# A layer of gated experts, attention and gated experts on one core: first rows on two queues, router held in TensorE, results stored in halves

## Time and profile before

| | |
|---|---|
| time, median of 3 runs | 471.35 us (469.79 to 471.42) |
| the profiled execution | 470.26 us, span 468.5 us, granted clock 0.993 |
| PE busy | 443.2 us, 95% of the span |
| PEld busy | 377.1 us, 80% |
| DVE busy | 353.5 us, 75% |
| ACT busy | 265.1 us, 57% |
| POOL busy | 281.6 us, 60% |
| moved by DMA | 53.62 MB, 114 GB/s |

### The profile page before, as it was taken

The page is one execution under the profiler, slowest core; times in us unless marked ns, Lnnn a source line. Parts: engine busy times, 40 slices in busy tenths (PEclk is TensorE's granted clock), DMA queues, the critical chain, the costliest instruction groups (busy, mean ns, idle before and its releaser), DMA issues.

```text
span 468.5 us, 9695 instructions
## 1 busy us (share of the span) xinstructions
PE 443.2 (95%) x2959; PEld 377.1 (80%) x2959; DVE 353.5 (75%) x1112; ACT 265.1 (57%) x596; POOL 281.6 (60%) x290
## 2 busy tenths in 40 slices
PE   7999999999999999999899999998899999999992
PEld 3878878888889888879787788887779888887872
DVE  4899996333688978999899999998899743454553
ACT  5965145555766657667533675654285565565630
POOL 4127556777775067713878850777574767763771
PEclk9999999999999999999999999999899999999998
DMA  7991143355422334311113321221443445553332
GB/s 225 366 341 46 55 127 123 99 174 135 127 84 83 92 95 112 109 44 52 57 53 90 96 70 51 69 80 63 124 129 104 135 148 148 152 160 102 95 102 63
DMA packets 74210, 53.62 MB, mean 114 GB/s; under 512 B 9648, under 2 KB 68784, under 8 KB 74160
## 3 DMA queue, kind: packets, MB, share of 16 engines
q1 hardware_dynamic: 65968, 36.19, 26.1%
q0 software_dynamic: 8192, 16.79, 12.1%
HBM read 26.81 MB, written 26.15 MB: 113 GB/s over the span
## 4 chain that ended last, share of the span: by engine, by line
PE 49%; DVE 22%; POOL 12%; issue 8%; DMA 4%; ACT 3%; SPq 0%; POOLq 0%; DVEq 0%; ACTq 0%
PE pool L899 13%; POOL x_sorted L1150 6%; PE gu L847 6%; PE pool L888 6%; PE gu L849 6%; PE gu L848 6%; POOL yg L1170 4%; PE pool L830 3%; DVE X L1236 2%; DVE hs L1213 2%; DVE hs L1217 2%; DVE stats L1247 2%; PE gu L806 1%; ACT xn L1059 1%; DVE xt_lo L1269 1%
## 5 line engine op out<-in xcount | busy, mean ns | idle before, releaser
L1150 POOL DMA_INDIRECT x_sorted<-xn,places x128 | 130.0, 1016 | 64.1 <-issue 33.0
L1170 POOL DMA_INDIRECT yg<-y_sorted,places x128 | 123.7, 966 | 54.2 <-issue 35.7
L1036 ACT ACTIVATE gs<-gu 128x512 f32<-128x512 f32 x124 | 72.4, 584 | 74.3 <-PE gu L849 37.6
L1213 DVE TENSOR_TENSOR hs<-gs,gu 128x512 f32<-128x512 f32 x92 | 60.6, 663 | 59.3 <-ACT gs L1036 58.4
L899 PE MATMUL pool<-w,hT 128*128 x708 | 96.9, 281 | 0.1
L899 PEld LDWEIGHTS pool<-w,hT 128*128 128x128 f32 x708 | 87.4, 191 | 11.3 <-issue 7.7
L847 PE MATMUL gu<-w,xbt_hi 128*128 x177 | 82.4, 465 | 1.5 <-DVE hs L1217 0.9
L849 PE MATMUL gu<-w,xbt_hi 128*128 x177 | 70.3, 397 | 0.0
L848 PE MATMUL gu<-w,xbt_lo 128*128 x177 | 70.2, 396 | 0.0
L1042 ACT ACTIVATE hT<-pool 128x512 f32<-128x512 f32 x92 | 53.3, 581 | 24.0 <-PE pool L888 22.7
L1017 ACT ACTIVATE ys<-pool 128x256 f32<-128x256 f32 x92 | 34.5, 375 | 46.8 <-PE pool L899 46.5
(11 more groups left out here) (137 smaller groups left out, 765.4 us busy)
## 6 DMA issues: line engine op xcount, KB each, us to landing
xb<-x_sorted SPq DMA_DIRECT2D x85, 128.0 KB, 2.4
y_sorted<-ys SPq DMA_DIRECT2D x85, 128.0 KB
x_sorted<-yg SPq DMA_DIRECT2D x6, 512.0 KB, 7.7
X<-x_dram SPq DMA_DIRECT2D x8, 256.0 KB, 4.6
x_sorted<-xn,places POOLq DMA_INDIRECT x128, 2.3
yg<-y_sorted,places POOLq DMA_INDIRECT x128, 2.7
out_dram<-X SPq DMA_DIRECT2D x8, 256.0 KB
raw<-gate_w_dram SPq DMA_DIRECT2D x4, 256.0 KB, 4.9
```

The source lines that it names most:

```text
L1036: nc.scalar.activation(dst, src, ACT.Silu).then_inc(silu_done, 1)
L1150: nc.gpsimd.indirect_dma_start(x_sorted[g], bass.IndirectOffsetOnAxis(places[g][:, k, t:t + 1], 0), xn[:, b, t % T], None).then_inc(scatte ...
L1170: nc.gpsimd.indirect_dma_start(yg[slot][:, k, t], None, y_sorted[g], bass.IndirectOffsetOnAxis(places[g][:, k, at:at + 1], 0)).then_inc(ga ...
L1213: v.tensor_tensor(hs[n % HB][:].rearrange("p (j i) -> p j i", j=2)[:, 0:k], gs[n % GB][:].rearrange("p (j i) -> p j i", j=2)[:, 0:k], bank ...
```

## The change

Ten edits in one.

1. The first batch's rows come in two transfers, tiles 0 and 1 from SP and tiles 2 and 3 from ACT's queue; two of the three shared weights move from SP's queue to ACT's. The third (`shared_down`) gets a semaphore of its own.
2. For the first batch of layer 1, tiles 2 and 3 are normalized on DVE (`norm_rest`) beside tiles 0 and 1 on ACT.
3. The logits hold the router in PE and stream the 512 rows of x: two matmuls for a batch. The router's 16 columns sit behind 96 zero columns, so that the member with index i of its group gets PSUM rows 32 i to 32 i + 15.
4. ACT adds the bias while it copies these rows to SBUF (`logit_rows`); for each group PE then turns the rows of all members in four transposes (`logit_turn`), and DVE adds the high and low halves (`halves`). `biased` on DVE goes.
5. In every `front` the wait for the low part moves from ahead of the three products to ahead of the third, which alone needs it; in R and KV units the order of the products changes for that.
6. A gather signals by pick, so that the first add waits for four gathers, not for eight.
7. The last add of a batch signals after its first half too, and the result is stored in two halves.
8. Lengths and needs of steps in the plan change.
9. URGENCY is a new string, so the order of the work on all engines and the paces are new.
10. POOL sets two more tensors to zero at its start; the table of biases moves from `tables` to the router's transfer.

```diff
-            load_x(0)
+            sp.dma_start(X[:, 0, 0:2], x[0].rearrange("(t p) d -> p t d", p=P)[:, 0:2]).then_inc(x_loaded[0], 16)
...
-            sp.dma_start(raw[:, E, 0:I], sgate).then_inc(shared_loaded, 16)
-            sp.dma_start(raw[:, E, I:GU], sup).then_inc(shared_loaded, 16)
...
         def _(act):
             once = Once(act)
+
+            act.dma_start(X[:, 0, 2:4], x[0].rearrange("(t p) d -> p t d", p=P)[:, 2:4]).then_inc(x_rest_loaded, 16)
+            act.dma_start(raw[:, E, 0:I], sgate).then_inc(shared_loaded, 16)
+            act.dma_start(raw[:, E, I:GU], sup).then_inc(shared_loaded, 16)
...
+            def norm_rest(l, b):
+                once.wait_ge(shift_done[l], b + 1)
+                for t in (2, 3):
+                    ins = v.tensor_scalar(xn[:, b, t], X[:, b, t], rstd[:, l, b, t:t + 1], shifts[:, l, b, t:t + 1],
+                                          ALU.mult, ALU.add)
+                ins.then_inc(norm_rest_done, 1)
...
-                dst = pool_ps[m]
-                hi, lo = xt_hi[plan.xt_of[l, b]], xt_lo[plan.xt_of[l, b]]
+                once.wait_ge(margin_set, 1)
+                row, i = ROWS * GROUPS[group_of(l, b)].index((l, b)), plan.xt_of[l, b]
+                pe.matmul(pool_ps[m][0:row + 2 * E], router_cut[:, MARGIN - row:], xt_hi[i][:], start=True, stop=False)
+                pe.matmul(pool_ps[m][0:row + E], router_cut[:, MARGIN - row:MARGIN + E], xt_lo[i][:],
+                          start=False, stop=True).then_inc(logits_ready[l], 1)
+
+            def logit_turn(g):
+                for l, b in GROUPS[g]:
+                    once.wait_ge(logits_read[l], b + 1)
+                once.wait_ge(squares_loaded, 16)
+                m = plan.misc["logit_turn", g]
+                take(m, halves_done, g + 1)
+                n = ROWS * len(GROUPS[g])
                 for t in range(T):
...
+                    mm = pe.transpose(pool_ps[m][:, t * P:t * P + n], logit_rows[0:n, t * P:(t + 1) * P], ident[0:n, 0:n])
+                mm.then_inc(logits_turned, 1)
...
+            def biased(l, b):
+                g = group_of(l, b)
+                row = ROWS * GROUPS[g].index((l, b))
+                once.wait_ge(logits_ready[l], b + 1)
...
+                wait(once, logits_turned, g)
+                rows = slice(row, row + 2 * E)
+                nc.scalar.activation(logit_rows[rows], misc("logits", l, b)[rows], ACT.Identity,
+                                     bias=bias_rows[rows, 0:1]).then_inc(logits_read[l], 1)
...
+            def halves(g):
+                once.wait_ge(logits_turned, g + 1)
...
+                for i in range(len(GROUPS[g])):
+                    ins = v.tensor_reduce(L[g][:, i * T:(i + 1) * T],
+                                          parts[:, :, i, 0:2 * E].rearrange("p t (r e) -> p t e r", r=2), AX.X, ALU.add)
+                ins.then_inc(halves_done, 1)
...
                     pe.matmul(dst[:, j], xbt_hi[r % 2][:, at], hi, start=True, stop=False)
-                    pe.matmul(dst[:, j], xbt_lo[r % 2][:, at], hi, start=False, stop=False)
-                    mm = pe.matmul(dst[:, j], xbt_hi[r % 2][:, at], lo, start=False, stop=True)
+                    pe.matmul(dst[:, j], xbt_hi[r % 2][:, at], lo, start=False, stop=False)
+                    once.wait_ge(xbt_lo_done, r + 1)
+                    mm = pe.matmul(dst[:, j], xbt_lo[r % 2][:, at], hi, start=False, stop=True)
...
-                if k == 0:
-                    once.wait_ge(gathered[b], 16 * 2 * T * (1 if l == 1 else 2))
-                    once.wait_ge(weigh_link, 3 * (g + 1))
+                once.wait_ge(gathered[b][k], 16 * T * (1 if l == 1 else 2))
+                once.wait_ge(weigh_link, 3 * (g + 1))
...
-                ins.then_inc(updated[b], 1)
+                    if t == T - 1 or (t == 1 and update(l, b, step) == LAST):
+                        ins.then_inc(updated[b], 1)
...
             def store_out(b):
-                once.wait_ge(updated[b], 7)
-                sp.dma_start(out[b].rearrange("(t p) d -> p t d", p=P), X[:, b]).then_inc(stored, 16)
+                for h in range(2):
+                    once.wait_ge(updated[b], LAST + h)
+                    half = slice(2 * h, 2 * h + 2)
+                    sp.dma_start(out[b].rearrange("(t p) d -> p t d", p=P)[:, half], X[:, b, half]).then_inc(stored, 16)
```

More of the change, by code:

```diff
@@ L29 @@
 EPS = 1e-5
+LAST = 7
+ROWS = 32
 LN_LINKS = 3
@@ L49 @@
[L49 to L53, removed]
@@ L142, in describe @@
             self.shared(3, b)
-            op(("out", b), "SP", 47, *(("add", 3, b, s) for s in ("first", "second", "shared")))
+            op(("out", b), "SP", 94, *(("add", 3, b, s) for s in ("first", "second", "shared")))
         for g in range(NG):
@@ L162, in norm @@
         op(("norm", l, b, 0), "ACT", 80, ("shift", l, b), *free)
-        op(("norm", l, b, 1), "ACT", 80, ("norm", l, b, 0))
-        op(("turn", l, b), "PE", 290 if (l, b) == (1, 0) else 45, ("norm", l, b, 1), ("squares",), lands=-245 * ((l, b) == (1, 0)))
+        if (l, b) == (1, 0):
+            op(("norm_rest", l, b), "DVE", 44, ("shift", l, b))
+        else:
+            op(("norm", l, b, 1), "ACT", 80, ("norm", l, b, 0))
+        normed = ("norm_rest", l, b) if (l, b) == (1, 0) else ("norm", l, b, 1)
+        op(("turn", l, b), "PE", 290 if (l, b) == (1, 0) else 44, ("norm", l, b, 0), normed, ("squares",),
+           lands=-245 * ((l, b) == (1, 0)))
         op(("hi", l, b), "ACT", 50, ("turn", l, b))
@@ L216, in route @@
         for n in range(2 * tiles(g)):
-            op(("scatter", g, n), "POOL", 126, ("place", g), *free, ("norm", *GROUPS[g][n // 2 // T], 1), lands=200)
+            op(("scatter", g, n), "POOL", 126, ("place", g), *free, ("turn", *GROUPS[g][n // 2 // T]), lands=200)
             free = (("scatter", g, n),)
@@ L332, in stage @@
         return group_of(1, b) + 0.5 if l == 2 else group_of(l, b)
-    ROUTING = ("clamp", "sigmoid", "inverse", "probs", "best", "second", "choose", "count", "based", "place", "table",
+    ROUTING = ("logit_turn", "halves", "clamp", "sigmoid", "inverse", "probs", "best", "second", "choose", "count", "based", "place", "table",
                "weigh")
@@ L905, in shared_down @@
                 once.wait_ge(h_done, nth_hidden["S", l, b, 1] + 1)
+                once.wait_ge(shared_down_loaded, 16)
                 m = plan.misc["sdown", l, b]
-                take(m, updated[b], update(l, b, "shared"))
+                take(m, updated[b], through(l, b, "shared"))
                 for t in range(T):
@@ L998, in _ @@
             multiply_ones(0, WARM)
-            run("PE", {"turn": xn_turn, "logits": logits, "count": count, "regs": find_experts, "pair_turn": pair_turn,
+            run("PE", {"turn": xn_turn, "logits": logits, "logit_turn": logit_turn, "count": count, "regs": find_experts, "pair_turn": pair_turn,
                        "front": front, "hidden_turn": hidden_turn, "down": down, "sdown": shared_down, "kv": kv,
@@ L1163, in gather @@
                     if old:
-                        once.wait_ge(updated[old[1]], update(*old, "second"))
+                        once.wait_ge(updated[old[1]], through(*old, "second"))
                     elif slot == YG - 1:
```

221 lines of the change are left out of this document (118 added, 103 removed).

## The result

The changed kernel takes 496.99 us (median of 4 runs, 496.18 to 497.72) against 471.34 for the kernel before: ratio 1.055, 95% interval 1.052 to 1.058. The forecast was 465.5 in a range of 459.5 to 470.5. The profiled executions differ as much: spans 494.5 and 468.5, 26.0 us.

The account below looks back on a forecast made before the run. It took PE's amount of work, with idle start and end, as the bound: logits -3.7, start -1.2, end -1.2, sum -6.1, less 1 us charge, from 470.26 gives 465.2; taken as 465.5 us, range 459.5 to 470.5.

Parts of the forecast that it names:

- The order as such: New URGENCY order on all engines: costed at zero, able to win or lose at most the middle's 13.7 us idle time.
- sign for a time above 469: Stated check on the measured time: above 469 us, the forecast would be wrong by its charge for keeping step.
- charge for keeping step: Before the first experts, scatters must start 3.8 us sooner out of a DVE 97% full: 1 us charged.
- handed back: Rival: first group's routing gets no earlier, so gains before 62 us become PE idle time; 467.5 us, chance 0.18.
- Logits: On PE, two wide products replace eight narrow ones per batch (-6.8 us), seven turns added (+3.1): net -3.7 us.
- The cheap bound of the turns: Lower limit for the seven logit_turn on PE: cost zero, in a range of 0 to 3.1 us, 3.1 taken.
- DVE and ACT: Bias and reduction work: DVE wins 2.1 us net; ACT gains 16 copies at 0.594 us, 9.5 us, hidden.
- Low part: Fronts on PE wait for the low part later: gain 0 to 0.5 us, taken as 0.
- The start: First batch's normalization split over ACT and DVE, rows landing earlier: first turn 1.2 us sooner, range 0.85 to 1.4.
- The end: After the last gather, four adds instead of eight (-1.15 us) and a store cut in two (0.05): -1.2 us.
- A longer routing chain: Rival: ACT copy, turns and reductions between logits and clamp add 0.9 to 3 us a group; 474 at 2.5, chance 0.09.

Follow-up runs that it names:

- e1: The changed kernel with one planned length, that of shared_down, put back from 179 to 182, so only order and paces differ: 467.76 us, ratio 0.995.
- e4: As e1, but each batch's two logit products issued twice (7.4 us more PE work, same result): 469.60 us, ratio 0.998.
- e6: As e1, with one URGENCY letter changed (moments of layer 3's seventh batch), leaving more shared work behind the last down: 462.21 us, ratio 0.982.
- e3: As e1, but every front waits for the low part ahead of its first product, as before the change: 467.88 us, ratio 0.994.
- e8: The changed kernel with one URGENCY letter changed (one down of the first group), so the fourth group's places come earlier: 493.07 us, ratio 1.047.
- e2: The kernel before, with none of the ten edits; only a front's planned length goes from 73 to 72, changing the order: 499.35 us, ratio 1.063.
- e9: As e6, with the end's edits undone in all batches (first adds wait for all eight gathers, batch stored whole): 534.55 us, ratio 1.134.
- e11: As e6, with 14 products of ones added behind PE's last product: 460.95 us, ratio 0.981.
- e12: As e6, with ACT's three transfers given back to SP and 14 products of ones behind PE's last: 462.93 us, ratio 0.984.
- e7: The changed kernel with one URGENCY letter changed (a layer 3 pair_turn), leaving four batches' shared work behind the last down: 480.68 us, ratio 1.020.
- e13: As e6, with the end's edits undone in layer 3's last batch alone (adds wait for all eight gathers, store whole): 463.88 us, ratio 0.987.

## Why the prediction was wrong

**The step that failed** is "The order as such I cost at zero: it can win no more than the 13.7 us of idle time in the middle, and can lose as much." The order lost 26 us. The bound took idle time in the middle for all that an order can change. An order also decides how much work PE has left for the 22 us in which routed work is over and the gathers run; the kernel before had 14.3 us of it there. That was to be seen ahead: PE idle for 8.5 us at the end and the last adds at 461 stood in the trace, but the time from the last `down` to the end was not read. And losing has no such bound: the idle time ahead of the last `down` grew by 15.7 us, about as much as all there was (16.8). Even a loss of the 13.7 us that the sentence allows would have been 484; no rival carried it, and the range ended at 470.5. The forecast's own sign for a time above 469 pointed at its charge for keeping step, and that was not the term.

**Charge for keeping step (1 us), handed back.** The first expert product came at 62.26 where 58 was foretold, and in every run on this change at 61.5 to 63.0 (before: 62.01). The work saved ahead of it moved other work forward and didn't bring the experts earlier. This rival's mechanism was right; its time, 467.5, is close to e1's.

**Logits, -3.7 us.** Right in size, near enough: 0.46 for the two products. The turns are 3.3 us as a group of instructions, but that counts the modelled ends; by the distance of starts, as the forecast counted, the seven take 2.6 (3.1 foretold). The 0.08 us of a wide product behind a narrow one stayed on PE's path, now with the logits. In time it is worth less than its sum, by e4. The cheap bound of the turns, zero, is out. The weight loads of the turns (PEld) took 136, 139 and 140 ns on the mean with 32, 64 and 96 rows, and 141 with 128 rows in the kernel before. The rule of the Trainium skill that the forecast weighed (TensorE: Matmul & The Clock Gate, LDWEIGHTS), by which a weight load's time doesn't go with its rows, agrees with that. The transposes still stand closer than the 0.11 us of the forecast, mostly 0.06 apart with 32 or 64 rows and 0.08 with 96; they also stream that many columns in place of 128.

**DVE and ACT.** The reduction took 0.217 (0.21), the copy 0.677 (0.594), `norm_rest` 0.60 for both (0.6). DVE's busy time, foretold to fall by 2.1 us, was 354.2 us in the changed kernel and 350.7 in e6, against 353.5 before.

**Low part: 0.** Right (e3).

**The start, -1.2 us.** Wrong in sign: 0.6 us later. The moved transfers were costed at nothing because the weights would arrive when they did; overlooked was that they pass the second batch's rows, behind which the first batch's `shift` stands. The late table load cost nothing beyond that: ACT, behind it, still waited 0.9 us for squares. The rule of the Trainium skill that spoke against the term (DMA: Bandwidth & Descriptors, Issuing engines are not separate DMA queues) agrees: the issues came earlier, and the second batch's rows were read 1.4 us later (6.69 against 5.33). The squares and first rows of the kernel before, which the forecast called in its favour, came through one queue and couldn't test it.

**The end, -1.2 us.** Four adds in place of eight came as told and won nothing that can be told: from the last gather's issue to the end it is 9.50 us before, 9.49 in the changed kernel and 9.34 to 9.42 in nine more traces with four adds. The path through adds and store was not the one that ended last.

**A longer routing chain** was on the right side and not the main cause (e8 made it shorter and won 3.9 us): `halves` to `places` took 16.0 us in e8 and 34.2 in the changed kernel, by what DVE's order put between.

Left is e6's 8 us, more than the 5.1 foretold: some 3 to 3.7 are the logits' term, nothing the start's or the end's, 1.3 less idle time. Some 3 us of less busy time stay open. By starts, and at full clock, the 531 products of the R units' fronts took 255 ns each in e6 and 260 before, 2.5 us in all; in e2, with the old order of products and another plan, it was 258. So the new order of the products in them may be part of it, which no run shows by itself.

## What to carry to other kernels

Where a list schedule makes the order, price an edit only with the order held: change a planned length by 0.01 us and see how far the time moves, read where the plan itself ends, and compare orders by the work that they leave for the time in which nothing else can run. Read the trace backwards from the end: find the last step behind which the chain is fixed, and ask of every edit whether that step comes earlier. An order made for a split wait may no longer be run with the old one (e9).

## What the runs showed of the hardware

The end of the program is not the end of its last store. In twelve executions the span ended 9.34 to 9.50 us after POOL's last gather was issued, with eight, four or no adds behind it, and also where PE's granted clock stayed at full until 2 us before the end (e11, e12). Where other work ended later (e2, e7, e9, e13) it ended 2.4 to 2.7 us after the last add. What POOL's queue does in those 9.4 us no trace shows. Squares, issued at 1.22 in both kernels, were read at 3.93 before and between 4.29 and 5.67 in the runs with a second queue's transfers beside them, so the second queue shared what there was. And a long wait of PE was paid twice here: behind 6.8 idle us in the changed kernel and 5.7 in e13 the granted clock was at half, and in e13 the work behind the wait took 3.78 us in place of 1.95.
